# Talking heads: mixed heads copied in two halves by two engines, scaling on GpSimd, mixing and scores interleaved

## The chip, the cores and the metric

One core of a Trainium2 chip runs the whole program in one launch. The metric is the device time of one execution in microseconds, lower being better. Five engines work from queues of their own and meet at semaphores only: TensorE (PE; its weight loads are listed as PEld), VectorE (DVE), ScalarE (ACT), GpSimd (POOL) and SyncE (SP, which issues most DMAs).

## What is computed

The reference runs five layers over 16 images, each with 36 patch tokens and 512 text tokens of width 192: patch embedding, a kernelised attention, a gated attention, attention with talking heads, and a mixture of nine experts. The change touches the fourth layer alone, after a layer norm and with a residual around it:

```python
attn = jnp.einsum("bhnd,bhmd->bhnm", q, k) * scale
attn = jnp.einsum("gh,bhnm->bgnm", th1_w, attn) + th1_b[None, :, None, None]
attn = jax.nn.softmax(attn, axis=-1)
attn = jnp.einsum("gh,bhnm->bgnm", th2_w, attn) + th2_b[None, :, None, None]
out = jnp.einsum("bhnm,bhmd->bhnd", attn, v)
```

There are 12 heads of width 16. Scores are mixed over the heads before the softmax (th1) and after it (th2), all in float32.

## The kernel before

The layer is the function `talking_heads` (from line 1811). It walks over 16 images of 550 rows (548 tokens and padding), each cut into 55 tiles of 10 queries, so 880 tiles. One loop over STEPS (line 1875) is written out on every engine: image b, place i of 0 to 54, tile n = 55 b + i. The work of one tile on its way:

- GpSimd, `qg` (L1956), one step ahead: the queries times th1 for each of the 12 output heads, in two instructions (two halves of 5 queries). Three buffers (SB = 3).
- TensorE, scores (L2273): queries times keys, 24 matmuls of 274 columns into two banks of PSUM, for tile n + 3 in step n.
- VectorE: the largest value of a row (max, L2070) and from it the bias of the exponential (nb, L2073), for tile n + 2.
- ScalarE: the exponential (L2162) out of PSUM into `P`, with the row sums `rs`.
- VectorE: the reciprocal of `rs` (L2083), and the scaling (L2087): the mixing matrix of th2 times that reciprocal, 60 columns, into `mixn`, for tile n + 1.
- TensorE, mixing (L2259): `P` as weights against `mixn`, 40 matmuls of 60 columns into two banks of PSUM (MB and MB + 1, one for each half of the queries), which turns the probabilities as well.
- ScalarE: one copy of both banks (L2152), 600 elements a partition, into `P2`. The mixing of the next tile waits for it (`p2_in`, L2250).
- TensorE, after each of six groups of tiles (places ENDS: 8, 17, 26, 35, 44, 54): the product with the values, 120 matmuls (L2298); VectorE takes its sums (oT, L2095).

The scores' banks are three pairs, handed out in order; `wait_bank` (L1891) makes TensorE wait until what was in a pair three uses ago has been taken.

Eleven places of an image carry items of the neighbouring images (SLOTS, L1818): Y (output projection of the image before), X, Q, K, V (norm and projections of the image after), R and L (turned tokens and logits for the experts). TensorE does an item after the scores of that step; VectorE empties Y, Q, K and L in its following step (`take`, L2032), ScalarE the others. VectorE also does the statistics of the next image's norm (L1981, L1984, L1989) at places 0 to 5 and of the last norm at places 9 to 14, and the normalisations (L1992) at 6, 7, 9, 10, 11, 15, 16 and 18. GpSimd raises their variances to the power -1/2 (L1963 at place 5, L1966 at place 14), once VectorE has signalled them.

On VectorE a step reads: max and nb of tile n + 2, the takes of the step before, reciprocal and scaling of tile n + 1, oT, statistics and normalisations. On ScalarE: the copy of tile n, the exponential of tile n + 2, its items. On GpSimd: `qg` of tile n + 4, then the powers. On TensorE: mixing of tile n, scores of tile n + 3, item, values.

Of the kernel before, what the change touches and what calls it, by code (L numbers as in the profile page):

```python
# [28 lines left out]
T = 5  # L29
# [19 lines left out]
QT = 10  # L49
QG = 9  # L50
NG = 5
# [1759 lines left out]
def talking_heads(k, A, logits, tokens, turned, wz, bz, xz):  # L1811
# [11 lines left out]
    with ExitStack() as ctx:  # L1823
# [25 lines left out]
        ready, gapped = sem("ready"), sem("gapped")  # L1849
# [41 lines left out]
        def wait_bank(eng, u):  # L1891

            for part, m in uses[u - SB] if u >= SB else ():
                if part == "T":
                    eng.wait_ge(prob, m + 1)
                elif part == "Z":
                    eng.wait_ge(summed, m + 1)
                else:
                    eng.wait_ge(taken[part[0]], count(part, m))
                    if part[0] == "Q":  # L1900
                        eng.wait_ge(spread, count(part, m))

# [6 lines left out]
        with nc.Block() as block:  # L1909
# [27 lines left out]
            def _(pool):  # L1937
# [8 lines left out]
                for b, i, n in STEPS:  # L1946
                    m = n + SB + 1
                    if is_tile(m):
# [11 lines left out]
                        ins.then_inc(qg_in, 1)  # L1960
                    if i == 5 and 0 <= b < B - 1:
# [11 lines left out]
            def _(dve):  # L1973
# [91 lines left out]
                for b, i, n in STEPS:  # L2065
                    if is_tile(n + 2):
# [5 lines left out]
                        dve.wait_ge(largest, m + 1)  # L2072
                        dve.tensor_scalar(nb[:, p:p + 1], nmx[:, p:p + 1], b1[:, 0:1], b1[:, 0:1], ALU.subtract, ALU.add) \  # L2073
                           .then_inc(bias, 1)
                    if before:
                        for part, im in items(*before):
                            if part[0] in "YQKL":
                                take(part, im, item_at[before])
                    if is_tile(n + 1):
# [24 lines left out]
            def _(act):  # L2104
# [66 lines left out]
            def _(pe):  # L2171
# [68 lines left out]

                TAIL = {"Y03": 4, "Ra": 7, "La": 1}
# [3 lines left out]
                for b, i, n in STEPS:  # L2245
                    if is_tile(n):
                        p = n % SB
                        pe.wait_ge(scaled, n + 1)
                        if n:
                            pe.wait_ge(p2_in, n)  # L2250
                        else:
                            pe.wait_ge(gapped, 2)
                        if i == 0 and b:
                            spare(SPARE[min(b, 2)], p)
                        for t in range(T):
                            for a in range(2):
                                for s in range(2):
                                    q = slice(64 * s, 64 * s + HQ + 1)
                                    ins = pe.matmul(PS[64 * a:64 * a + KP, MB + s, t * HQ:(t + 1) * HQ], P[q, p, a, t * KP:(t + 1) * KP],  # L2259
                                                    mixn[q, p], start=True, stop=True)  # L2260
                        ins.then_inc(mixed, 1)
                    if is_tile(n + SB):
                        m = n + SB
                        p, bank, im = m % SB, 2 * (tile_at[m] % SB), m // NTILE
                        pe.wait_ge(qg_in, m + 1)
                        if m % NTILE == 0:
                            pe.wait_ge(taken["K"], count("K2", im))
                        wait_bank(pe, tile_at[m])
                        for c in range(NC):
                            for a in range(2):  # L2270
                                s = slice(a * PC, (a + 1) * PC)
                                for o, w in ((0, 64), (64, MR)):
# [598 lines left out]
```

## Time and profile before

| | us |
|---|---|
| median of 3 runs (lowest, highest) | 4380.58 (4378.49, 4381.98) |
| the profiled execution | 4380.37 |
| its span, first to last instruction | 4378.6 |
| PE busy in the span | 4176.6 (95%) |
| PEld, DVE, ACT, POOL busy | 3286.3, 2534.3, 2188.3, 1717.9 |

Times in a timeline are microseconds from the first instruction. A line joins neighbouring instructions of one kind; the number after the engine's idle time in brackets names what ended it, and "issue" stands for idle time that no semaphore in the profile explains. Matmuls overlap, and their ends are modelled: a start is exact, an end is not. In the groups by line, the number after the busy time is the mean of one instruction in ns.

### The profile page before, as it was taken

What the parts mean: (1) busy time and instruction counts of PE and PEld (TensorE: products, weight loads), DVE (VectorE), ACT (ScalarE), POOL (GpSimd) and SP (SyncE); (2) the same over time, 40 slices, a digit from 0 to 9 for tenths busy, and PEclk for the clock granted to TensorE, in tenths of its full rate; (3) what the DMA queues carried; (4) which work ended last, traced back from release to release, by engine and by line L of the source; (5) the groups of instructions that cost most, each with busy time, mean ns of one, the idle gap of its engine ahead of it and who ended that gap; (6) DMA issues with size and microseconds to landing.
All of it is one profiled execution on the core that took longest, in us unless ns stands there. A gap on an engine that the chain in (4) does not pass through costs nothing. (4 is left out here: it accounts for less than half of the span.)

```text
span 4378.6 us, 201182 instructions
## 1 busy us (share of the span) xinstructions
PE 4176.6 (95%) x88202; PEld 3286.3 (75%) x88202; DVE 2534.3 (58%) x7273; ACT 2188.3 (50%) x5051; POOL 1717.9 (39%) x2794
## 2 busy tenths in 40 slices
PE   6998998999989999999999999999999999999998
PEld 4555665766657777777877877787778777999997
DVE  5776886666655655566565556555655554432332
ACT  3453443555536555555555555555555553213443
POOL 2223435776743333333333333333333331002565
PEclk8999999999999999999999999999999999999999
DMA  5112210000000000100000000000000001332333
GB/s 114 25 34 47 48 33 7 1 2 1 1 14 4 16 5 14 24 16 4 16 16 16 4 16 16 16 4 16 16 16 4 16 16 38 77 88 65 66 67 50
DMA packets 122908, 114.73 MB, mean 26 GB/s; under 512 B 64000, under 2 KB 110594, under 8 KB 122042
## 3 DMA queue, kind: packets, MB, share of 16 engines
q1 hardware_dynamic: 94646, 66.47, 6.5%
q0 software_dynamic: 16768, 23.59, 3.0%
q10 hardware_dynamic: 10628, 11.80, 1.2%
q8 instruction: 706, 11.57, 1.1%
q14 instruction: 160, 1.31, 0.1%
HBM read 59.89 MB, written 41.48 MB: 23 GB/s over the span
## 5 line engine op out<-in xcount | busy, mean ns | idle before, releaser
L2273 PE MATMUL PS<-th_kT,th_qg 64*61 64x274 f32 (+1 forms) x21120 | 1461.1, 393 | 9.4 <-issue 7.0
L1956 POOL TENSOR_TENSOR th_qg<-th_qT,w_th_th 128x180 f32<-128x180 f32 x1760 | 849.9, 505 | 1355.6 <-PE PS L2273 1344.3
L2152 ACT ACTIVATE th_P<-PS 119x600 f32<-119x600 f32 x880 | 649.6, 738 | 849.9 <-PE PS L2259 849.5
L2273 PEld LDWEIGHTS PS<-th_kT,th_qg 64*61 64x61 f32 (+1 forms) x21120 | 879.8, 132 | 204.5 <-issue 35.2
L2070 DVE TENSOR_REDUCE th_nmx<-PS 125x1 f32<-125x548 f32 x880 | 640.3, 728 | 632.5 <-PE PS L2273 632.0
L2259 PEld LDWEIGHTS PS<-th_mixn,th_P 61*55 61x55 f32 x35200 | 672.6, 125 | 173.4 <-issue 66.9
L2259 PE MATMUL PS<-th_mixn,th_P 61*55 61x60 f32 x35200 | 708.0, 214 | 48.3 <-issue 40.4
L2162 ACT ACTIVATE th_P<-PS,th_nb 125x548 f32<-125x548 f32 x880 | 623.1, 708 | 105.7 <-DVE th_nb L2073 105.5
L1388 POOL TENSOR_SCALAR ga_P<-ga_P,ga_rw 110x110 f32<-110x110 f32 (+4 forms) x240 | 264.9, 1115 | 160.5 <-DVE ga_rw L1556 159.7
L2073 DVE TENSOR_SCALAR th_nb<-th_nmx,w_th_b 125x1 f32<-125x1 f32 x880 | 240.2, 273 | 32.2
L2298 PE MATMUL PS<-th_P,th_v 119*32 119x90 f32 (+1 forms) x11520 | 250.4, 244 | 1.1 <-ACT th_P L2152 0.8
L2298 PEld LDWEIGHTS PS<-th_P,th_v 119*32 119x32 f32 x11520 | 229.6, 110 | 29.1 <-issue 27.9
L2087 DVE TENSOR_SCALAR th_mixn<-w_th_mix,th_rs 125x60 f32<-125x60 f32 x880 | 233.0, 265 | 31.6
L2508 POOL DMA_INDIRECT ex_cx<-ex_tokens,ex_token_of x77 | 80.6, 1046 | 340.7 <-DVE ex_b L2685 250.7
L1617 ACT ACTIVATE ga_PT<-PS 110x440 f32<-110x440 f32 (+3 forms) x240 | 102.5, 427 | 198.3 <-PE PS L1702 196.1
L1030 PE MATMUL PS<-w_pf_wK,pf_xT 64*110 64x456 f32 x960 | 196.9, 557 | 1.5 <-ACT pf_xT L925 1.5
L2447 ACT ACTIVATE ez_h<-PS,ex_bz 128x550 f32<-128x550 f32 x96 | 69.0, 720 | 241.2 <-PE PS L2711 241.2
L2523 POOL DMA_INDIRECT out_h<-ex_cy,ex_token_of x77 | 130.6, 1697 | 132.1 <-DMA out_h<-ex_cy,ex_token_of 111.6
L2162 ACT ACTIVATION_READ_ACCUMULATOR th_P<-PS,th_nb 125x1 f32 x880 | 177.6, 202 | 0.0
L1079 PE MATMUL PS<-w_pf_wQ,pf_xT 64*110 64x360 f32 x960 | 166.9, 480 | 10.8 <-DVE X L901 6.4
L2434 ACT ACTIVATE ez_h<-PS,ex_cb 128x128 f32<-128x128 f32 x462 | 127.8, 376 | 77.5 <-PE PS L2782 75.8
L2772 PE MATMUL PS<-ex_cxT,ex_wz 64*128 64x128 f32 x2772 | 165.2, 275 | 1.0 <-ACT ez_h L2434 1.0
(369 smaller groups left out, 6291.8 us busy)
## 6 DMA issues: line engine op xcount, KB each, us to landing
pf_xT<-pf_spill SPq DMA_DIRECT2D x32, 412.5 KB, 5.5
ex_tokens<-th_xn SPq DMA_DIRECT2D x124, 82.5 KB
pf_spill<-pf_xT SPq DMA_DIRECT2D x16, 412.5 KB, 3.7
ex_turned<-th_rT SPq DMA_DIRECT2D x16, 412.5 KB, 3.7
ex_x<-ex_turned SPq DMA_DIRECT2D x32, 206.2 KB, 4.1
out_h<-X SPq DMA_DIRECT2D x16, 330.0 KB
ex_w<-in_L_ffn_W ACTq DMA_DIRECT2D x18, 288.0 KB
ex_w<-in_L_ffn_W ACTq DMA_DIRECT2D x8, 576.0 KB
```

The costliest lines, as they stand in the source:

```text
L1030: ins = pe.matmul(PS[0:R, p + a, 0:HM + D], xT[half, slot(u), c, cols(u)], wK[half, c, :], start=c == 0, stop=c == NC - 1)
L1079: ins = pe.matmul(PS[0:R, p + a, 0:HM + C], xT[half, qslot(u), c, cols(u)], wQ[half, c, :], start=c == 0, stop=c == NC - 1)
L1388: pool.tensor_scalar(P[:, n % 4, u, 0:keys(t)], P[:, n % 4, u, 0:keys(t)], rw[:, n % 4, u:u + 1], None, ALU.mult).then_inc(scaled, 1)
L1956: ins = pool.tensor_tensor(qg[:, m % SB, :, 64 * s:64 * s + HQ].rearrange("p c (h n) -> p c h n", n=QH), qT[:, im % 2, :, at + s * QH:at + ...
L2070: dve.tensor_reduce(nmx[:, p:p + 1], PS[0:MR, bank:bank + 2, 0:HK], AX.XY, ALU.max, negate=True) \
L2073: dve.tensor_scalar(nb[:, p:p + 1], nmx[:, p:p + 1], b1[:, 0:1], b1[:, 0:1], ALU.subtract, ALU.add) \
L2087: dve.tensor_scalar(mixn[:, p], mix[:], rs[:, p:p + 1], None, ALU.mult).then_inc(scaled, 1)
L2152: act.activation(P2[:, :, :, at * QT:(at + 1) * QT].rearrange("p t h (s n) -> p s (t h) n", s=2), PS[0:PK, MB:MB + 2, 0:VO].rearrange("p s ...
L2162: act.activation(P[:, p, :, 0:HK], PS[0:MR, bank:bank + 2, 0:HK], ACT.Exp, bias=nb[:, p:p + 1], accum_out=rs[:, p:p + 1]).then_inc(prob, 1)
L2259: ins = pe.matmul(PS[64 * a:64 * a + KP, MB + s, t * HQ:(t + 1) * HQ], P[q, p, a, t * KP:(t + 1) * KP], mixn[q, p], start=True, stop=True)
L2273: ins = pe.matmul(PS[o:w, bank + a, 0:HK], qg[s, p, c, o:w], kT[s, im % 2, c, :], start=c == 0, stop=c == NC - 1)
L2298: ins = pe.matmul(PS[32 * j:32 * j + 32, bank, c * nq:(c + 1) * nq], v[0:PK, b % 2, t].rearrange("p h d -> p (h d)")[:, at:at + 32], P2[:, ...
```

## The change

Four things change in `talking_heads`. The copy of the mixed heads becomes two: ScalarE copies bank MB, the first 5 queries, and VectorE bank MB + 1, the other 5; both wait for the mixing (and, at the first tile of a group, for the last value product) through the new helper `part_of`, and TensorE waits for both (`p2_in` and the new `p2_half`) before the next mixing and before the value product. The scaling goes from VectorE to GpSimd, behind the query product of the step. On VectorE the reciprocal now stands ahead of nb, and the takes stand behind the half copy. On TensorE, mixing and scores of a step are cut: key blocks 0 to 2 of 5 of the mixing, chunk 0 of 3 of the scores, blocks 3 and 4 of the mixing, chunks 1 and 2 of the scores. Matmuls, buffers and DMAs are the same.

```diff
+        def part_of(eng, n):
+
+            g = min(n % NTILE // QG, NG)
+            at = n % NTILE - g * QG
+            eng.wait_ge(mixed, n + 1)
+            if at == 0 and n:
+                eng.wait_ge(pv, n // NTILE * GROUPS + g)
+            return at
...
@@ gpsimd @@
                         ins.then_inc(qg_in, 1)
+                    if is_tile(n + 1):
+                        m = n + 1
+                        p = m % SB
+                        pool.wait_ge(recip, m + 1)
+                        if m >= SB:
+                            pool.wait_ge(mixed, m - SB + 1)
+                        pool.tensor_scalar(mixn[:, p], mix[:], rs[:, p:p + 1], None, ALU.mult).then_inc(scaled, 1)
                     if i == 5 and 0 <= b < B - 1:
...
@@ vector @@
                            .then_inc(largest, 1)
-                        dve.wait_ge(largest, m + 1)
-                        dve.tensor_scalar(nb[:, p:p + 1], nmx[:, p:p + 1], b1[:, 0:1], b1[:, 0:1], ALU.subtract, ALU.add) \
-                           .then_inc(bias, 1)
-                    if before:
-                        for part, im in items(*before):
-                            if part[0] in "YQKL":
-                                take(part, im, item_at[before])
                     if is_tile(n + 1):
                         m = n + 1
                         p = m % SB
                         dve.wait_ge(prob, m + 1)
                         dve.reciprocal(rs[:, p:p + 1], rs[:, p:p + 1]).then_inc(recip, 1)
-                        dve.wait_ge(recip, m + 1)
-                        if m >= SB:
-                            dve.wait_ge(mixed, m - SB + 1)
-                        dve.tensor_scalar(mixn[:, p], mix[:], rs[:, p:p + 1], None, ALU.mult).then_inc(scaled, 1)
+                    if is_tile(n + 2):
+                        m = n + 2
+                        p = m % SB
+                        dve.wait_ge(largest, m + 1)
+                        dve.tensor_scalar(nb[:, p:p + 1], nmx[:, p:p + 1], b1[:, 0:1], b1[:, 0:1], ALU.subtract, ALU.add) \
+                           .then_inc(bias, 1)
+                    if is_tile(n):
+                        at = part_of(dve, n)
+                        dve.tensor_copy(P2[:, :, :, at * QT + QH:(at + 1) * QT].rearrange("p t h n -> p (t h) n"),
+                                        PS[0:PK, MB + 1, 0:VO].rearrange("p (x n) -> p x n", n=QH)).then_inc(p2_half, 1)
+                    if before:
+                        for part, im in items(*before):
+                            if part[0] in "YQKL":
+                                take(part, im, item_at[before])
...
@@ scalar @@
-                        g = min(n % NTILE // QG, NG)
-                        at = n % NTILE - g * QG
-                        act.wait_ge(mixed, n + 1)
-                        if at == 0 and n:
-                            act.wait_ge(pv, n // NTILE * GROUPS + g)
-                        act.activation(P2[:, :, :, at * QT:(at + 1) * QT].rearrange("p t h (s n) -> p s (t h) n", s=2),
-                                       PS[0:PK, MB:MB + 2, 0:VO].rearrange("p s (x n) -> p s x n", n=QH), ACT.Copy).then_inc(p2_in, 1)
+                        at = part_of(act, n)
+                        act.activation(P2[:, :, :, at * QT:at * QT + QH].rearrange("p t h n -> p (t h) n"),
+                                       PS[0:PK, MB, 0:VO].rearrange("p (x n) -> p x n", n=QH), ACT.Copy).then_inc(p2_in, 1)
...
@@ tensor: the two loops become helpers mix_pieces(n, pieces) and score_pieces(m, chunks) @@
                         pe.wait_ge(scaled, n + 1)
                         if n:
                             pe.wait_ge(p2_in, n)
+                            pe.wait_ge(p2_half, n)
...
-                        for t in range(T):
-                            for a in range(2):
-                                for s in range(2):
...
-                        ins.then_inc(mixed, 1)
+                        mix_pieces(n, range(0, 3))
                     if is_tile(n + SB):
...
                         wait_bank(pe, tile_at[m])
-                        for c in range(NC):
...
-                        ins.then_inc(score, 1)
+                        score_pieces(m, range(0, 1))
+                    if is_tile(n):
+                        mix_pieces(n, range(3, T)).then_inc(mixed, 1)
+                    if is_tile(n + SB):
+                        score_pieces(n + SB, range(1, NC)).then_inc(score, 1)
...
                         pe.wait_ge(p2_in, n + 1)
+                        pe.wait_ge(p2_half, n + 1)
```

## Rows read from the trace of the kernel before

**Rows 1.** busy time by stretch: us, each engine's busy time (count), PEclk, DMA, GB/s

```profile
1290.50:3662.50 2372.00, 2312.35 (x70512) 1855.27 (x70514) 1397.68 (x4275) 1349.67 (x2822) 881.10 (x1784) 1.00 0.05 13
```

**Rows 2.** timeline, one step: start us, us, engine, line, operation, count, [idle before]

```profile
2035.68 0.71 PE L2259 MATMUL PS<-th_mixn,th_P 61*55 61x60 f32 x40
2035.94 0.73 DVE L2070 TENSOR_REDUCE th_nmx<-PS 125x1 f32<-125x548 f32 x1 [1.70 <-PE PS L2273]
2036.21 1.58 PE L2273 MATMUL PS<-th_kT,th_qg 64*61 64x274 f32 x24
2036.47 0.74 ACT L2152 ACTIVATE th_P<-PS 119x600 f32<-119x600 f32 x1 [1.18 <-PE PS L2259]
2036.71 0.27 DVE L2073 TENSOR_SCALAR th_nb<-th_nmx,w_th_b 125x1 f32<-125x1 f32 x1
2036.90 0.15 DVE L2083 RECIPROCAL th_rs<-th_rs 125x1 f32<-125x1 f32 x1
2037.09 0.25 DVE L2087 TENSOR_SCALAR th_mixn<-w_th_mix,th_rs 125x60 f32<-125x60 f32 x1
2037.25 0.35 DVE L1981 BATCH_NORM_STATS2 th_st<-X 110x6 f32<-110x192 f32 x1
2037.60 0.71 PE L2259 MATMUL PS<-th_mixn,th_P 61*55 61x60 f32 x40
```

**Rows 3.** who waited for whom, weight loads: us, times, longest

```profile
PEld PS L2259 <- issue: 66.9, 147, 1.4
PEld PS L2273 <- issue: 35.2, 80, 1.5
```

**Rows 4.** timeline: mixing of a step 27, scores of a step 9

```profile
2104.46 0.59 PE L2259 MATMUL PS<-th_mixn,th_P 61*55 61x60 f32 x28 [0.29 <-issue]
2206.38 0.20 PEld L2273 LDWEIGHTS PS<-th_kT,th_qg 64*64 64x64 f32 x7 [0.30 <-issue]
```

**Rows 5.** DMA queues of the page: packets, MB, share

```profile
q8 instruction: 706, 11.57, 1.1%
```

**Rows 6.** groups by shape, ACT, DVE and GpSimd: busy us, mean ns, idle before

```profile
L2128 ACT ACTIVATE th_v<-PS 128x192 f32<-128x192 f32 x16 | 5.3, 331 | 15.1 <-PE PS L2217 15.1
L2054 DVE COPY th_kT<-PS 128x274 f32<-128x274 f32 x15 | 6.7, 444 | 13.8 <-PE PS L2224 13.8
L2052 DVE COPY th_kT<-PS 128x548 f32<-128x548 f32 x15 | 10.9, 729 | 33.3 <-PE PS L2224 32.3 <-PE PS L2207 0.9
L2095 DVE TENSOR_TENSOR th_oT<-PS,w_th_one 128x180 f32<-128x180 f32 x80 | 27.7, 346 | 133.1 <-PE PS L2298 133.1
L1388 POOL TENSOR_SCALAR ga_P<-ga_P,ga_rw 110x110 f32<-110x110 f32 x48 | 27.4, 582 | 42.0 <-DVE ga_rw L1556 42.0
```

**Rows 7.** timeline, steps 5 to 7: GpSimd, scaling, mixing of tile 7

```profile
2048.31 1.17 POOL L1963 TENSOR_TENSOR th_rstd<-th_ve,mhalf 110x5 f32<-110x5 f32 x1 [5.60 <-DVE th_ve L1989]
2049.45 1.95 POOL L1956 TENSOR_TENSOR th_qg<-th_qT,w_th_th 128x180 f32<-128x180 f32 x4
2049.61 0.85 DVE L2087 TENSOR_SCALAR th_mixn<-w_th_mix,th_rs 125x60 f32<-125x60 f32 x1
2050.51 0.70 PE L2259 MATMUL PS<-th_mixn,th_P 61*55 61x60 f32 x36 [0.21 <-DVE th_mixn L2087]
```

**Rows 8.** timeline, step 4: mixing after slot 3, take of Y03

```profile
2044.33 0.75 PE L2259 MATMUL PS<-th_mixn,th_P 61*55 61x60 f32 x40
2044.44 0.96 DVE L2037 TENSOR_TENSOR X<-PS,X 110x768 f32<-110x768 f32 x1 [1.70 <-PE PS L2195]
```

**Rows 9.** timeline, steps 14 to 16: mixing, variance, power, mixing

```profile
2070.82 0.75 PE L2259 MATMUL PS<-th_mixn,th_P 61*55 61x60 f32 x40
2071.58 0.17 DVE L1989 TENSOR_SCALAR th_ve<-th_mv 110x5 f32<-110x5 f32 x1
2071.83 1.17 POOL L1966 TENSOR_TENSOR th_rstd<-th_ve,mhalf 110x5 f32<-110x5 f32 x1 [3.48 <-DVE th_ve L1989]
2074.71 0.70 PE L2259 MATMUL PS<-th_mixn,th_P 61*55 61x60 f32 x40
```

More of the change, by code:

```diff
@@ L1847, in sem @@
             return nc.alloc_semaphore("th_" + name)
-        ready, gapped = sem("ready"), sem("gapped")
+        ready, gapped, p2_half = sem("ready"), sem("gapped"), sem("p2_half")
         var, powed, xn_in = sem("var"), sem("powed"), sem("xn_in")
@@ L2239, in stream, with mix_pieces, score_pieces @@
                         pe.matmul(PS[:, bank, 0:2 * D], ident[0:C, :], wk[0:C].rearrange("p c n -> p (c n)"), start=True, stop=True)
+                def mix_pieces(n, pieces):
+                    p = n % SB
+                    for t in pieces:
+                        for a in range(2):
+                            for s in range(2):
+                                q = slice(64 * s, 64 * s + HQ + 1)
+                                ins = pe.matmul(PS[64 * a:64 * a + KP, MB + s, t * HQ:(t + 1) * HQ], P[q, p, a, t * KP:(t + 1) * KP],
+                                                mixn[q, p], start=True, stop=True)
+                    return ins
+                def score_pieces(m, chunks):
+                    p, bank, im = m % SB, 2 * (tile_at[m] % SB), m // NTILE
+                    for c in chunks:
+                        for a in range(2):
+                            s = slice(a * PC, (a + 1) * PC)
+                            for o, w in ((0, 64), (64, MR)):
+                                ins = pe.matmul(PS[o:w, bank + a, 0:HK], qg[s, p, c, o:w], kT[s, im % 2, c, :],
+                                                start=c == 0, stop=c == NC - 1)
+                    return ins
                 TAIL = {"Y03": 4, "Ra": 7, "La": 1}
@@ L2246, in _ @@
                     if is_tile(n):
-                        p = n % SB
                         pe.wait_ge(scaled, n + 1)
@@ L2253, in _ @@
                         if i == 0 and b:
-                            spare(SPARE[min(b, 2)], p)
-                        for t in range(T):
-                            for a in range(2):
-                                for s in range(2):
-                                    q = slice(64 * s, 64 * s + HQ + 1)
-                                    ins = pe.matmul(PS[64 * a:64 * a + KP, MB + s, t * HQ:(t + 1) * HQ], P[q, p, a, t * KP:(t + 1) * KP],
-                                                    mixn[q, p], start=True, stop=True)
-                        ins.then_inc(mixed, 1)
+                            spare(SPARE[min(b, 2)], n % SB)
+                        mix_pieces(n, range(0, 3))
                     if is_tile(n + SB):
                         m = n + SB
-                        p, bank, im = m % SB, 2 * (tile_at[m] % SB), m // NTILE
                         pe.wait_ge(qg_in, m + 1)
                         if m % NTILE == 0:
-                            pe.wait_ge(taken["K"], count("K2", im))
+                            pe.wait_ge(taken["K"], count("K2", m // NTILE))
                         wait_bank(pe, tile_at[m])
-                        for c in range(NC):
-                            for a in range(2):
-                                s = slice(a * PC, (a + 1) * PC)
-                                for o, w in ((0, 64), (64, MR)):
-                                    ins = pe.matmul(PS[o:w, bank + a, 0:HK], qg[s, p, c, o:w], kT[s, im % 2, c, :],
-                                                    start=c == 0, stop=c == NC - 1)
-                        ins.then_inc(score, 1)
+                        score_pieces(m, range(0, 1))
[3 more added lines that the diff above has]
+                        score_pieces(n + SB, range(1, NC)).then_inc(score, 1)
                     if (b, i) in item_at:
```

## The prediction, made before the change was run

> **What bounds the kernel now.** I read the busy times by stretch first, then one step in order of time, then who waits for whom, then prices. [...]
>
> The plain step shows how near the others are [rows 2]. Mixing starts at 2035.68, the scores at 2036.21, the next mixing at 2037.60: 0.53 us of mixing, 1.39 of scores, 1.92 in all; 880 such tiles are 1690 us, the items of the slots and the value products the rest. With 0 at the start of mixing, the max starts at 0.26, nb at 1.03, the reciprocal at 1.22, the scaling at 1.41, ending at 1.66; ScalarE's copy runs from 0.79 (0.26 after the mixing is out) to 1.53. The next VectorE instruction can start 0.09 before the one ahead of it ends (the scaling ends at 2037.34, statistics start at 2037.25). Both releases of the next mixing come only 0.26 to 0.39 us ahead of it.
>
> The list of waits gives the holes that are there: the weight loads of mixing sat idle 66.9 us and those of the scores 35.2 us for "issue", no semaphore at all [rows 3]. The trace has them within a block: 0.29 us ahead of the last 28 of 40 mixing matmuls in a step 27, 0.30 in the middle of the scores' weight loads in a step 9 [rows 4]. PE's instruction stream comes in 706 transfers of 11.57 MB, 16 KB each [rows 5]; I take these holes for late instructions. At most 102 us is to be had from them.
>
> **The change, part by part.**
>
> *Plain step: 0.* ScalarE's half is 300 elements: between 192 at 0.33 us [rows 6] and 600 at 0.74 [rows 2], 0.42. VectorE's half is like the 274-element copy at 0.44 [rows 6]: 0.47. GpSimd's scaling of 60 columns isn't in the trace; its nearest rows are 0.25 on VectorE [rows 2] and 0.58 for GpSimd's 110 columns [rows 6]; I take 0.45, nearer the row of that engine. TensorE's pieces are 0.32, 0.46, 0.21 and 0.93, still 1.92 together. The last mixing is out at 0.99, so both copies start at 1.25: ScalarE's half ends at 1.67. VectorE does max, reciprocal, nb (0.26 + 0.73 + 0.07 + 0.19 = 1.25), then its half until 1.72, free for the next at 1.63. The reciprocal now ends near 1.1, GpSimd's scaling at 1.6, earlier than VectorE's 1.66. Against 1.92 there is 0.20 left for the half; where the scaling was waited for, mixing came 0.05 after its end [rows 7], so I count 0.1 as slack. The cover is thin: without it a plain step pays up to 0.05, and 44 steps without an item in each of 16 images are 700. Bounds 0 to +35 us; 0 taken, since 0.20 is over 0.05.
>
> *Steps after an item: +2.2 us an image.* Here VectorE also empties an item's banks (take). Before, that stood ahead of the reciprocal and ran while the mixing did: Y03's add began at 2044.44 beside the mixing of 2044.33 [rows 8]. Now it stands behind the half, which waits for this tile's last mixing; queued behind that wait are the take, the sums of the values (oT), the statistics and the next max. They begin at 1.63 after the mixing's start, and the next max is due at 0.26 + 1.92 = 2.18: with T of such work it is T - 0.55 late. The half after it is as late, and with 0.1 of slack TensorE stalls T - 0.65, before the mixing three steps behind the item. Y03: 0.96 - 0.09 [rows 8] and statistics of 0.35 [rows 2] (0.27 and 0.08 for their sum): T 1.22, 0.57. Q0, Q1, Q2: two copies of 0.44 [rows 6] and a bubble, 0.92; after Q0 and Q2 also oT, 0.35 - 0.09 [rows 6]: 0.53, 0.27, 0.53. K01 with La: 0.73 - 0.09 [rows 6] and 0.09: 0.08. Together 1.98. Step 9 would lose 0.5 in the same way (Y4, oT, statistics, a normalisation: 1.16), but it has a hole of 0.3 of its own [rows 4]: 0.21, and without that cover 0.51. K2 with Lb and oT is 0.36, 0.09 and 0.26, hardly over 0.65: left out. Sum 2.19.
>
> *GpSimd's queue: +1.24 us an image.* The scaling now waits for VectorE's reciprocal, and behind it stands the next query product, two instructions, 0.96; 1.41 a step in 1.92 is no bound, and the products have three buffers. Not so where the powers stand in the queue. Step 5: the power starts at 2048.31, lasts 1.17, the product of the next step runs until 2050.41 [rows 7]; the scaling for tile 7 then ends at 2050.86 and mixing starts at 2050.91, not at 2050.51, where it now waits for a VectorE scaling stretched to 0.85 by the side of GpSimd's product [rows 7]: +0.40, and 0.04 as VectorE is later. Step 14: the statistics stand behind the half of a tile whose mixing starts at 2070.82 [rows 9]; half from 2072.07, last statistics at 2072.45, the variance 0.21 later, the power 0.25 after that (as 2071.58 to 2071.83), the product 1.14 on, 0.96 and 0.45 long: 2075.46, mixing of tile 16 at 2075.51 and not 2074.71 [rows 9]: +0.80. SP's queue is not passed; GpSimd issues no DMA here until the stage ends.
>
> *Weave: -8 us.* It moves no work, but mixing takes 80 instructions (40 matmuls [rows 2] and their weight loads) in 0.53 us and the scores 48 in 1.39. In the last two fifths of the mixing, TensorE's queue can now fill during the first third of the scores. Two fifths of 66.9 are 27 us; a third of that is gained, as the instruction transfers stay as long. Bounds 0 (nothing) to -68 (two thirds of all 102).
>
> [...]
>
> *Other waits.* One more semaphore for TensorE before mixing and before the value products: both stand after ScalarE's, at work of 1.72 against 1.92 (0). ScalarE gains 0.3 a step, off the path (0).
>
> **Sum.** (2.19 + 1.24) x 15 images = +51. Step 27, which Q0 would delay by 0.53, has the hole of [rows 4] in it: -0.3 x 15 = -5. Weave -8. Net +38. The profiled execution took 4380.37 us (its span of 4378.6 and 1.8 around it), 0.2 below the median of the runs, so 4380.4 + 38 = **4418 us**.
>
> **Rivals.**
> 1. *Faster: the holes for instructions close.* They are set by how densely mixing eats instructions; the weave puts 64 into each half of a step, the stream keeps up, -55 of the 102 comes back, and half of the new waits fall where holes were (+25): 4350 (4337 at -68, 4357 at -48). It decides once the weave saves more than the waits cost. For it: holes lie within mixing [rows 4]. Against: the same 128 instructions per 1.92 us, transfers of the same length.
> 2. *No change.* The late VectorE work falls into holes that are there, and only GpSimd's +1.24 x 15 = 19 is left, less 8 to 20 of the weave: 4380 to 4391, 4384. For it: holes of 102 us are as large as all new waits. Against: the new ones come at steps of their own, and of those reckoned here only steps 9 and 27 showed a hole.
> 3. *Slower still.* The half gates plain steps too: 0.25 from its end to the mixing and not 0.1 gives 0.05 x 700 = 35: 4453. For it: 0.20 of room. Against: the 0.05 of [rows 7].
> 4. The change not doing what it says would be a mixing that still waits for one 600-element copy; the diff leaves none.
>
> **How the numbers follow.** Forecast (4395 to 4438) 0.50, rival 1 0.21, rival 2 0.13, rival 3 0.16. About 0.2% (9 us) is what a measurement can tell. Faster 0.21, same 0.12, and slower 0.67 (forecast, rival 3 and the top of rival 2). Range 4356 to 4454: it takes in the two slower cases, rival 2 and rival 1 up to its weaker end; the forecast's own is 4395 to 4438.
>
> **What would show it.** Right: mixing waits on VectorE's half after the steps of Y03, Q0 to Q2; the weight loads of mixing wait on GpSimd's scaling some 15 times after step 5 and 15 after step 14; plain steps stay at 1.92; "issue" idle of mixing and scores falls by under 30 us. Wrong: "issue" idle falling by over 50 (rival 1), or every plain step near 1.97 (rival 3), or GpSimd's scaling far from 0.45.

## The result, and the profile after

The changed kernel takes 4434.53 us (median of 4 runs, 4430.71 to 4436.11) against 4381.28 us of the kernel before beside it: ratio 1.0117, 95% interval 1.0105 to 1.0129. That is 53 us slower. The forecast was 4418 us, its range 4356 to 4454. Timed beside the kernel before on a second chip (4366 us there), the ratio was 1.0136, interval 1.0120 to 1.0153. All experiments below ran on chips where the kernel before took 4358 to 4366 us; they are compared by their ratios to it, the change itself at 1.0136. Its own ratio moved by 0.0019 from one chip to the other, so a smaller difference between two experiments (0.0019 is 8 us) decides nothing.

The profiled execution took 4436.11 us, 55.7 us more than that of before. The page's first lines, and the stage in the busy times by stretch (columns as in [rows 1]):

```profile
span 4434.4 us, 202173 instructions
PE 4225.1 (95%) x88202; PEld 3238.4 (73%) x88202; DVE 2655.3 (60%) x7273; ACT 1943.2 (44%) x5051; POOL 2065.0 (47%) x3674
```

```profile
1290.50:3718.50 2428.00, 2361.26 (x70535) 1806.62 (x70535) 1515.09 (x4276) 1104.89 (x2822) 1232.12 (x2667) 1.00 0.05 12
```

The stage went from 2372.00 [rows 1] to 2428.00 us, so the whole loss is in it, at the same granted clock of 1.00. ScalarE gave up 245 us of work, VectorE took 117 and GpSimd 351. The groups by line price the three new instructions, which were estimated at 0.45, 0.42 and 0.47 us:

```profile
L1976 POOL TENSOR_SCALAR th_mixn<-w_th_mix,th_rs 125x60 f32<-125x60 f32 x880 | 384.9, 437 | 1161.5 <-DVE th_rs L2092 1089.9
L2167 ACT ACTIVATE th_P<-PS 119x300 f32<-119x300 f32 x880 | 403.8, 459 | 1182.6 <-PE PS L2262 1182.6
L2101 DVE COPY th_P<-PS 119x300 f32<-119x300 f32 x880 | 414.1, 471 | 611.2 <-PE PS L2262 606.8
```

A plain step, to be laid beside [rows 2] (timeline; mixing is now L2262, scores L2272):

```profile
2171.99 0.52 PE L2262 MATMUL PS<-th_mixn,th_P 61*55 61x60 f32 x24
2172.26 0.73 DVE L2086 TENSOR_REDUCE th_nmx<-PS 125x1 f32<-125x548 f32 x1 [0.45 <-PE PS L2272]
2172.31 0.67 PE L2272 MATMUL PS<-th_kT,th_qg 64*64 64x274 f32 x8
2172.78 0.41 PE L2262 MATMUL PS<-th_mixn,th_P 61*55 61x60 f32 x16
2172.90 0.15 DVE L2092 RECIPROCAL th_rs<-th_rs 125x1 f32<-125x1 f32 x1
2172.99 1.13 PE L2272 MATMUL PS<-th_kT,th_qg 64*64 64x274 f32 x16
2173.15 0.43 POOL L1976 TENSOR_SCALAR th_mixn<-w_th_mix,th_rs 125x60 f32<-125x60 f32 x1 [0.69 <-DVE th_rs L2092]
2173.26 0.43 ACT L2167 ACTIVATE th_P<-PS 119x300 f32<-119x300 f32 x1 [0.78 <-PE PS L2262]
2173.26 0.48 DVE L2101 COPY th_P<-PS 119x300 f32<-119x300 f32 x1
2173.59 0.71 ACT L2177 ACTIVATE th_P<-PS,th_nb 125x548 f32<-125x548 f32 x1
2173.92 0.27 PE L2262 MATMUL PS<-th_mixn,th_P 61*55 61x60 f32 x5
```

The pieces start at 0, 0.32, 0.79 and 1.00, the half ends at 1.75, the next mixing comes at 1.93. The plain step is as drawn. So the loss sits in particular steps, and the list of waits is the next view to read, beside [rows 3]:

```profile
PEld PS L2262 <- POOL th_mixn L1976: 109.6, 321, 1.3
PEld PS L2262 <- issue: 107.7, 415, 1.1
PEld PS L2272 <- issue: 63.2, 174, 1.3
PE PS L2262 <- issue: 22.2, 55, 0.9
PE PS L2262 <- POOL th_mixn L1976: 15.7, 27, 0.8
PE PS L2262 <- DVE th_P L2101: 3.6, 15, 1.1
```

It misleads three times. The 109.6 us on GpSimd's scaling are mostly the short idle time that a weight load has in any step whose last release is the scaling: in the run below in which no step is late for it, it is still 63.9. VectorE's half, which mixing was to wait for after the steps of Y03 and Q0 to Q2, is named 15 times only, ahead of place 11; in step 28, shown below, the list names the scaling, which ends 0.24 us before the next mixing starts, and the half ends only 0.15 before it. And the idle time for "issue", where a fall was forecast, rose from 66.9 to 107.7 us for the weight loads of mixing and from 35.2 to 63.2 for those of the scores [rows 3]; without the weave they are 49.3 and 34.3. For the scores, "issue" turns out to hide a semaphore.

What tells more is the length of each step, by its place in the image (from the start of one mixing to the next, in each trace; median over images 1 to 14, us; "all three" and the others are the experiments below):

```
place           24    33    42     5     6    15    28    10    38    30
before         1.92  1.94  1.92  1.92  2.30  1.92  1.92  2.09  1.92  1.92
after          2.21  2.21  2.21  2.45  2.90  2.84  2.43  2.37  2.38  1.93
no weave       1.92  1.92  1.92  1.98  2.90  2.38  1.97  1.92  1.92  1.92
takes early    2.21  2.21  2.21  2.23  2.86  2.84  1.93  2.10  2.09  1.93
power moved    2.21  2.21  2.21  2.23  1.93  2.21  2.43  2.44  2.24  1.93
early + power  2.21  2.21  2.21  2.23  1.93  2.26  1.93  2.17  2.10  1.93
but five       1.99  1.99  1.99  2.01  1.93  1.99  1.93  2.17  2.35  1.93
all three      1.92  1.92  1.92  1.92  1.92  1.92  1.92  1.92  1.92  1.92
```

Places 24, 33 and 42 grew by 0.27 to 0.29 us with no late work behind them. The timeline of place 24 of one image after, and then of the same place without the weave:

```profile
2118.92 0.71 ACT L2177 ACTIVATE th_P<-PS,th_nb 125x548 f32<-125x548 f32 x1
2119.28 0.49 PE L2262 MATMUL PS<-th_mixn,th_P 61*55 61x60 f32 x24
2119.52 0.20 ACT L2177 ACTIVATION_READ_ACCUMULATOR th_P<-PS,th_nb 125x1 f32 x1
2119.83 0.23 PEld L2272 LDWEIGHTS PS<-th_kT,th_qg 64*64 64x64 f32 x8 [0.19 <-issue]
2119.86 0.69 PE L2272 MATMUL PS<-th_kT,th_qg 64*64 64x274 f32 x8
```

```profile
2094.35 0.71 ACT L2177 ACTIVATE th_P<-PS,th_nb 125x548 f32<-125x548 f32 x1
2094.95 0.20 ACT L2177 ACTIVATION_READ_ACCUMULATOR th_P<-PS,th_nb 125x1 f32 x1
2095.18 0.70 PE L2262 MATMUL PS<-th_mixn,th_P 61*55 61x60 f32 x40
2095.70 1.57 PE L2272 MATMUL PS<-th_kT,th_qg 64*64 64x274 f32 x24
```

Banks are handed out in turn, three pairs. The item of slot 22 takes one, so the scores of step 24 get the pair of the tile scored in step 22, two steps back and not three, and `wait_bank` waits for that tile's exponential. After the change this exponential ends 0.44 us after the mixing starts (2119.72), since it stands behind a half copy that starts only when the woven mixing is out; the first third of the scores is due at 0.32 and starts at 0.58. Without the weave the exponential ends at 2095.15, before the mixing, and the scores are due at 0.52. The same holds two steps behind every slot that carries an item without a value product: 3, 13, 22, 31, 40, so places 5, 15, 24, 33, 42.

### The profile page after: what moved, and what is told of

It is laid out like the page before. It is cut to its first block and busy times, and to the rows that moved or that the text cites. A ratio compares the mean times of both kernels' runs of the same rounds, so it can differ in the third digit from the quotient of the medians.

```text
span 4434.4 us, 202173 instructions
## 1 busy us (share of the span) xinstructions
PE 4225.1 (95%) x88202; PEld 3238.4 (73%) x88202; DVE 2655.3 (60%) x7273; ACT 1943.2 (44%) x5051; POOL 2065.0 (47%) x3674
## 3 DMA queue, kind: packets, MB, share of 16 engines
q8 instruction: 706, 11.57, 1.1%
## 5 line engine op out<-in xcount | busy, mean ns | idle before, releaser
L2272 PE MATMUL PS<-th_kT,th_qg 64*61 64x274 f32 (+1 forms) x21120 | 1648.7, 394 | 18.7 <-issue 12.5
L2262 PEld LDWEIGHTS PS<-th_mixn,th_P 61*55 61x55 f32 x35200 | 842.1, 125 | 328.5 <-POOL th_mixn L1976 109.6
L2262 PE MATMUL PS<-th_mixn,th_P 61*55 61x60 f32 x35200 | 904.2, 215 | 44.7 <-issue 22.2
L1976 POOL TENSOR_SCALAR th_mixn<-w_th_mix,th_rs 125x60 f32<-125x60 f32 x880 | 384.9, 437 | 1161.5 <-DVE th_rs L2092 1089.9
L2167 ACT ACTIVATE th_P<-PS 119x300 f32<-119x300 f32 x880 | 403.8, 459 | 1182.6 <-PE PS L2262 1182.6
L2272 PEld LDWEIGHTS PS<-th_kT,th_qg 64*61 64x61 f32 (+1 forms) x21120 | 767.2, 132 | 152.4 <-issue 63.2
L2101 DVE COPY th_P<-PS 119x300 f32<-119x300 f32 x880 | 414.1, 471 | 611.2 <-PE PS L2262 606.8
```

Of the source, the lines that this page charges most:

```text
L1976: pool.tensor_scalar(mixn[:, p], mix[:], rs[:, p:p + 1], None, ALU.mult).then_inc(scaled, 1)
L2101: dve.tensor_copy(P2[:, :, :, at * QT + QH:(at + 1) * QT].rearrange("p t h n -> p (t h) n"), PS[0:PK, MB + 1, 0:VO].rearrange("p (x n) -> ...
L2167: act.activation(P2[:, :, :, at * QT:at * QT + QH].rearrange("p t h n -> p (t h) n"), PS[0:PK, MB, 0:VO].rearrange("p (x n) -> p x n", n=Q ...
L2272: ins = pe.matmul(PS[o:w, bank + a, 0:HK], qg[s, p, c, o:w], kT[s, im % 2, c, :], start=c == 0, stop=c == NC - 1)
```

## The experiments

**Is it the weave?** In the changed kernel, mixing and scores are each in one piece again.

```diff
-                        mix_pieces(n, range(0, 3))
+                        mix_pieces(n, range(T)).then_inc(mixed, 1)
...
-                        score_pieces(m, range(0, 1))
-                    if is_tile(n):
-                        mix_pieces(n, range(3, T)).then_inc(mixed, 1)
-                    if is_tile(n + SB):
-                        score_pieces(n + SB, range(1, NC)).then_inc(score, 1)
+                        score_pieces(m, range(NC)).then_inc(score, 1)
```

> The changed kernel with the mixing of a tile in one piece again and the scores in one piece behind it; halves, GpSimd's scaling and the late takes stay. Theory A (the weave costs time): in the changed kernel the first third of the scores starts 0.32 us after the mixing and not 0.53, and at places 5, 15, 24, 33 and 42, two steps behind an item, it then waits some 0.27 us for the exponential that has its bank; and both half copies start 0.46 later, and all that stands behind them on VectorE with them. Without the weave the five waits go (1.35 us an image, 20 us over 15), the steps 5, 28 and 37 lose most of what they gained (about 1 us an image, 15 us), the power of place 14 starts 0.46 earlier (7 us), and some 7 us of instruction holes come back: 4434.5 - 35, about 4399. Theory B (as the prediction had it, the weave gains 8 us and costs nothing): 4442. Theory C (holes for instructions dominate): 4460 or more.

Measured: ratio 1.0028, interval 1.0017 to 1.0040, against 1.0136 for the whole change on such a chip: the weave costs 0.0108, 47 us (0.0089 or 39 against the first 1.0117), more than the 35 of theory A. Places 24, 33, 42, 10 and 38 are back at 1.92, 5 and 28 nearly so, place 15 fell by 0.46. Place 6 stays at 2.90: the power's. The takes of places 5, 10 and 28 stand as late in VectorE's queue as before and now cost 0.06 us at most: the mixing that they stand behind is out at 0.52 and not at 1.00. So here late takes cost only beside the weave, and the 47 us hold both.

**Is it the takes?** The takes move up, between nb and the half copy.

```diff
                            .then_inc(bias, 1)
+                    if before:
+                        for part, im in items(*before):
+                            if part[0] in "YQKL":
+                                take(part, im, item_at[before])
                     if is_tile(n):
                         at = part_of(dve, n)
...
-                    if before:
...
```

> The changed kernel with VectorE's takes (Y, Q, K, L) put between nb and the half copy instead of behind it. Theory A: the late takes cost what places 10 to 12, 28 and 37 gained and part of place 5 (about 1.3 us an image), the rest of the loss being bank waits of the weave and GpSimd's powers: 4434.5 - 20, about 4415, with places 24, 33 and 42 still at 2.21 us and place 15 at 2.84. Theory B (the prediction's: all 2.19 us an image are the takes'): 4434.5 - 33, about 4402. Theory C (the waits come from GpSimd's queue whatever VectorE does): 4434.

Measured: 1.0106, interval 1.0089 to 1.0123, 0.0030 or 13 us under the change (5 against the first 1.0117). Place 28 fell by 0.50, 10 by 0.27, 5 by 0.22; 24, 33, 42 and 15 stayed, as theory A had it. By places that is 1.0 us an image, 15 us, as the timing has it. Theory B's 33 us are out. Place 38 fell by 0.29 too, but not for its take: one pair of neighbouring instructions of TensorE there starts 0.66 us apart after the change, 0.35 with the takes early and 0.05 without the weave (means), a hole of the kind that the last experiments are about. Place 28 after the change shows how a late take costs (VectorE, TensorE and GpSimd; the Q0 of slot 26):

```profile
2130.82 0.47 DVE L2101 COPY th_P<-PS 119x300 f32<-119x300 f32 x1 [4.15 <-PE PS L2262]
2131.21 0.88 DVE L2061 COPY th_qT<-PS 64x275 f32<-64x275 f32 x2
2131.50 0.52 PE L2262 MATMUL PS<-th_mixn,th_P 61*55 61x60 f32 x24
2132.16 0.23 PEld L2272 LDWEIGHTS PS<-th_kT,th_qg 64*64 64x64 f32 x8 [0.27 <-issue]
2132.19 0.69 PE L2272 MATMUL PS<-th_kT,th_qg 64*64 64x274 f32 x8 [0.16 <-issue]
2132.38 0.72 DVE L2086 TENSOR_REDUCE th_nmx<-PS 125x1 f32<-125x548 f32 x1
2133.26 0.43 POOL L1976 TENSOR_SCALAR th_mixn<-w_th_mix,th_rs 125x60 f32<-125x60 f32 x1 [5.36 <-DVE th_rs L2092]
2133.32 0.46 DVE L2101 COPY th_P<-PS 119x300 f32<-119x300 f32 x1
2133.90 0.53 PEld L2262 LDWEIGHTS PS<-th_mixn,th_P 61*55 61x55 f32 x23 [0.37 <-POOL th_mixn L1976]
2133.93 0.63 PE L2262 MATMUL PS<-th_mixn,th_P 61*55 61x60 f32 x23
```

VectorE stood 4.15 us with the item's bank full, waiting for the mixing, and took it afterwards, until 2132.09. The scores of step 28 need that bank: due at 2131.82, they start at 2132.19. The late max then delays reciprocal, scaling and half as well, and the next mixing starts 0.15 after the half.

**Is it the power?** The statistics start earlier, so that GpSimd's powers fall into steps 3 and 13, in which TensorE has an item to do.

```diff
-                    if i == 5 and 0 <= b < B - 1:
+                    if i == 3 and 0 <= b < B - 1:
...
-                    if i == 14 and b >= 1:
+                    if i == 13 and b >= 1:
...
-                    if i <= T:
+                    if im == 0 and i <= T:
                         stat_of(im, 0, i)
+                    if im and i <= T - 2:
+                        stat_of(im, 0, i + 2)
...
-                    if 9 <= i <= 9 + T:
+                    if 8 <= i <= 8 + T:
...
-                        stat_of(im, 1, i - 9)
+                        stat_of(im, 1, i - 8)
...
+                    if b + 2 < B and i >= NTILE - 2:
+                        stat_of(b + 2, 0, i - NTILE + 2)
```

> The changed kernel with the statistics of the next norm two places earlier (53, 54, 0 to 3) and those of the last norm one place earlier (8 to 13), so that GpSimd's two powers of 1.2 us stand at places 3 and 13, steps of 5.1 and 3.7 us in which GpSimd idles, and not at 5 and 14. Theory A (the power stands ahead of a query product and the scaling, and mixing waits for that): place 6 falls from 2.90 to about 2.3 and place 15 from 2.84 to about 2.2 (the bank wait of 0.27 stays), 1.25 us an image: 4434.5 - 19, about 4415. Theory B (the late VectorE sets these steps, not the power): less than 6 us gained, 4429 or more.

Measured: 1.0100, interval 1.0080 to 1.0120, 0.0036 or 16 us under the change (7 against the first 1.0117). Place 6 fell to 1.93, place 15 to 2.21; places 10 and 16 grew by 0.07 and 0.20. What went is seen in step 15 after the change, beside [rows 9]:

```profile
2096.97 1.20 POOL L1982 TENSOR_TENSOR th_rstd<-th_ve,mhalf 110x5 f32<-110x5 f32 x1 [1.56 <-DVE th_ve L2005]
2098.14 0.97 POOL L1965 TENSOR_TENSOR th_qg<-th_qT,w_th_th 128x180 f32<-128x180 f32 x2
2099.09 0.51 POOL L1976 TENSOR_SCALAR th_mixn<-w_th_mix,th_rs 125x60 f32<-125x60 f32 x1
2099.65 0.40 PEld L2262 LDWEIGHTS PS<-th_mixn,th_P 61*55 61x55 f32 x24 [0.92 <-POOL th_mixn L1976]
```

Power, product, scaling, mixing: the queue that the prediction had drawn. The mixing before it started at 2096.81.

**All three together.** What is left of the change are the halves and the scaling on GpSimd.

> The three edits together: no weave, takes ahead of the half copy, powers at places 3 and 13. Halves and GpSimd's scaling are all that is left of the change. Theory A (the loss is those three and nothing else): 4381 give or take 8, that is no better than the kernel before, since the halves and the scaling on GpSimd shorten no step that TensorE bounds. Theory B (halves and GpSimd's scaling cost by themselves, in each plain step): 4395 or more. Theory C (shorter VectorE and ScalarE queues gain something once the rest is out of the way): 4370 or less.

Measured: 0.9978, interval 0.9968 to 0.9988, 4356.14 us against 4366.09; on the 4381 us from which the theories reckon that is 4372, just under theory A's 4373 and above theory C's 4370. Each of the ten places above is at 1.92, so the three edits hold the loss of these places; why the time is even below that of the kernel before is taken up with the last experiments. Here is the wait on the scaling that is left in a kernel in which it costs nothing:

```profile
PEld PS L2268 <- POOL th_mixn L1976: 63.9, 328, 1.2
```

**The change once more, and the weave with nothing else against it.** The changed kernel was timed again beside the next three runs; then the early takes and the moved powers with the weave kept.

> The changed kernel itself once more, so that it has been timed beside the kernel before on a second chip, on which the kernel before took 4366 us and not 4381. Theory A: the loss comes from waits between engines, at the same places of each image, and is 48 to 55 us here too (ratio 1.011 to 1.0125). Theory B: part of it is holes for instructions, which differ from chip to chip; then the ratio moves by more than 0.002.

Measured: 1.0136, interval 1.0120 to 1.0153; it differs from 1.0117 by 0.0019, just under the 0.002 that was to speak for theory B, and it lies above theory A's 1.011 to 1.0125: it decides for neither.

> The changed kernel with the takes ahead of the half copy and the powers at places 3 and 13; the weave stays. It differs from the run with all three edits (0.9978 of before) by the weave alone. Theory A (the weave costs five bank waits of 0.28 us an image, 21 us, and little else once the takes and the powers are out of its way): 0.9978 + 0.005, about 1.003. Theory B (the edits add up as they were measured one by one, -0.0011 and -0.0017 from 1.0117): 1.0089. Theory C (the weave costs nothing by itself): 0.998.

Measured: 1.0057, interval 1.0042 to 1.0072, between theories A and B. Takes and powers, worth 13 and 16 us one by one, are worth 34 together. The weave by itself costs 1.0057 - 0.9978 = 0.0079, another 34 us. The five places make 1.5 us an image of it, 23 us.

**Are the halves worth anything?** The run with all three edits, with ScalarE's single copy; and the kernel before with the powers moved.

```diff
-                        act.activation(P2[:, :, :, at * QT:at * QT + QH].rearrange("p t h n -> p (t h) n"),
-                                       PS[0:PK, MB, 0:VO].rearrange("p (x n) -> p x n", n=QH), ACT.Copy).then_inc(p2_in, 1)
+                        act.activation(P2[:, :, :, at * QT:(at + 1) * QT].rearrange("p t h (s n) -> p s (t h) n", s=2),
+                                       PS[0:PK, MB:MB + 2, 0:VO].rearrange("p s (x n) -> p s x n", n=QH), ACT.Copy).then_inc(p2_in, 1)
...
-                        dve.tensor_copy(P2[:, :, :, at * QT + QH:(at + 1) * QT].rearrange("p t h n -> p (t h) n"),
-                                        PS[0:PK, MB + 1, 0:VO].rearrange("p (x n) -> p x n", n=QH)).then_inc(p2_half, 1)
...
```

> The run with all three edits (no weave, early takes, moved powers), and ScalarE copies both banks again in one instruction, as before; VectorE has no half. What is left of the change is the scaling on GpSimd and the reciprocal ahead of nb. Theory A (ScalarE's copy was never the bound, the halves gain nothing): the same within 0.0012 as with halves, 0.9978. Theory B (the earlier exponential frees the scores' banks sooner, the halves gain): 1.000 or more. Theory C (VectorE's half ends 0.19 later than ScalarE's whole copy and holds work behind it, the halves cost): 0.996 or less.

> The kernel before with the statistics and the powers moved to places 3 and 13 and nothing else. In the kernel before only place 6 shows the power (2.30 us and not 1.92, VectorE's scaling stretched beside GpSimd's product). Theory A: 0.38 us an image is gained, 6 us, ratio 0.9987; then some 4 us of what the run with all three edits gained (0.9978) are from the scaling on GpSimd and the halves. Theory B: 0.9978, all of that gain is the moved power and nothing of it the change's. Theory C: no change, 1.000.

Measured: 1.0004 (0.9994 to 1.0013) and 1.0000 (0.9990 to 1.0010). At face value the halves would gain 0.0026, theory B's figure, and the scaling on GpSimd nothing. But between the run with the halves and the one without, the plain steps are alike (1.92), and places 0, 7, 8 and 17, which are 1.4 us shorter together with the halves, stand against 9, 11, 16 and 40, which are 1.4 longer (means). Most of this is holes that changed places, as the last two runs show them: 1.0 of the first 1.4 at places 0 and 7, 1.1 of the second at 9, 11 and 40. At place 16 the halves cost 0.26: VectorE's half, late behind two normalisations, ends 0.15 before the next mixing. With the powers moved in the kernel before, place 6 fell from 2.30 to 1.92; these 6 us do not show in its time.

**Is there room on VectorE for both?** All three edits, the scaling back on VectorE behind the reciprocal.

```diff
-                        pool.tensor_scalar(mixn[:, p], mix[:], rs[:, p:p + 1], None, ALU.mult).then_inc(scaled, 1)
...
                         dve.reciprocal(rs[:, p:p + 1], rs[:, p:p + 1]).then_inc(recip, 1)
+                        dve.wait_ge(recip, m + 1)
+                        if m >= SB:
+                            dve.wait_ge(mixed, m - SB + 1)
+                        dve.tensor_scalar(mixn[:, p], mix[:], rs[:, p:p + 1], None, ALU.mult).then_inc(scaled, 1)
...
```

> The run with all three edits (no weave, early takes, moved powers; 0.9978 of before), and the scaling back on VectorE, right behind the reciprocal; the halves stay. Theory A (VectorE has no room for both): in a plain step the max ends 0.99 after the mixing starts, the reciprocal 1.10, the scaling 1.35, nb 1.54, the half about 2.0, past the 1.92 of the step; some 700 plain steps grow by 0.15 us or a little more, 105 us and up: ratio 1.022 or more. Theory B (the half fits, since VectorE's chain shifts against TensorE's): 0.998 to 1.002, and the scaling need not have moved.

Measured: 1.0084, interval 1.0068 to 1.0099: 0.0106 or 46 us over the run with all three edits, in the direction of theory A and less than half its size. One step of its timeline:

```profile
2463.25 0.75 PE L2265 MATMUL PS<-th_mixn,th_P 61*55 61x60 f32 x40
2464.35 0.25 DVE L2093 TENSOR_SCALAR th_mixn<-w_th_mix,th_rs 125x60 f32<-125x60 f32 x1
2464.70 0.46 DVE L2106 COPY th_P<-PS 119x300 f32<-119x300 f32 x1
2465.31 0.75 PE L2265 MATMUL PS<-th_mixn,th_P 61*55 61x60 f32 x40
```

The half ends at 1.91, the next mixing starts 0.15 later, at 2.06. Only part of the plain steps are so long; place 30 is 2.09, places 24, 33 and 42 are 2.04, place 38 stays at 1.93. So VectorE can carry the half only once the scaling has left it; the two parts of the change belong together.

**Are the five places what the weave costs?** The run that kept the weave, unwoven at five places.

```diff
-                        mix_pieces(n, range(0, 3))
+                        cut = T if i in (5, 15, 24, 33, 42) else 3
+                        ins = mix_pieces(n, range(cut))
+                        if cut == T:
+                            ins.then_inc(mixed, 1)
...
-                    if is_tile(n):
-                        mix_pieces(n, range(3, T)).then_inc(mixed, 1)
+                    if is_tile(n) and cut < T:
+                        mix_pieces(n, range(cut, T)).then_inc(mixed, 1)
```

> The run with early takes and moved powers that kept the weave (1.0057 of before), with the weave undone at places 5, 15, 24, 33 and 42 alone. Theory A (there the scores' first third comes two steps behind an item, too early for the exponential that has its bank): these five steps fall from 2.21 to 2.32 us to some 1.93, 1.5 us an image, 22 us: 1.0057 - 0.005, about 1.0007; what is left of the weave's 0.0079 is 0.003. Theory B (the bank wait only stands where TensorE would wait anyway): 1.0045 or more.

Measured: 1.0095, interval 1.0082 to 1.0109: slower, where 1.0007 was expected. Yet the five places fell nearly as expected, to 1.99 to 2.01. In exchange place 17 grew by 0.98 us and place 44 by 1.01 (means). Step 17, PE alone:

```profile
2383.18 0.52 PE L2268 MATMUL PS<-th_mixn,th_P 61*55 61x60 f32 x21
2384.68 0.31 PE L2268 MATMUL PS<-th_mixn,th_P 61*55 61x60 f32 x3 [0.98 <-issue]
2384.81 0.69 PE L2278 MATMUL PS<-th_kT,th_qg 64*64 64x274 f32 x8
```

This is a hole of 1 us within one block of matmuls, where the kernel has no semaphore. I counted the starts of TensorE's instructions, semaphore instructions included. In this trace 75 gaps between neighbouring starts are over 0.4 us in images 1 to 14, and all 75 fall on the same position modulo 256, that is on cuts between the 16 KB transfers of [rows 5] (64 bytes an instruction, by 11.57 MB and the 180,758 instructions counted before). The packets of that queue show what is waited for: in every trace here, TensorE goes on after such a gap 1.19 to 1.68 us after a 16 KB transfer has landed, while about half of the cuts without a gap are crossed later than that. So the hole is a wait for instructions. Gaps over 0.25 us at these cuts add up to 76.5 us; in the run that kept the weave everywhere they were 59.0. So 15 us of bank waits were removed and 17.5 us of holes came up elsewhere; the timing (0.0038 more) is worse still, which these two profiles don't settle. By idle time of the mixing matmuls, first the run with the weave everywhere, then this one:

```profile
PE PS L2268 <- issue: 25.4, 73, 0.9
```

```profile
PE PS L2268 <- issue: 42.2, 91, 1.1
```

**Do the holes depend on the cuts alone?** All three edits, with 32 more and with 32 fewer one-column spare matmuls ahead of image 1.

```diff
-    SPARE = (39, 43, 14)
+    SPARE = (39, 75, 14)
```

(and 11 for 75).

> The run with all three edits (0.9978 of before), with 32 more one-column spare matmuls ahead of image 1, so that from there on TensorE's instruction stream is cut into its 16 KB transfers 64 instructions later in every image. Theory A (the holes without a semaphore are set by where these cuts fall): they leave places 9, 11, 13 and 40 and turn up elsewhere, and the time moves by more than 6 us one way or the other. Theory B (the holes belong to the places, whatever the cut): the same places and 0.9978 within 0.0014.

> The run with all three edits (0.9978 of before) with 32 fewer one-column spare matmuls ahead of image 1 (11 and not 43), so that the cuts between TensorE's instruction transfers come 64 instructions earlier; with 32 more it was 1.0017. Theory A (any shift moves the holes; the three points scatter by more than 0.003, so that a difference of 0.2% between kernels whose instruction streams are cut differently says nothing of the edit): outside 0.9978 give or take 0.0014 in either direction. Theory B (0.9978 is what the schedule is worth and the run with 32 more was the odd one): within it.

Measured: 1.0017 (1.0007 to 1.0027) and 1.0007 (0.9998 to 1.0016). The two expectations speak of 64 instructions. The traces have 64 more and 64 fewer matmuls, each with a weight load, so the cuts moved by 128 instructions, half a transfer, forward and back, and that is the same place: 450 of 490 cuts fall on the same instruction of the same step in both, none where the run with all three edits has one, and the holes agree (place 18 at 2.94 us in both, 1.96 with all three edits alone). This is one shift, timed twice. With 32 more, place 9 falls from 2.82 to 1.96 us, 11 from 2.37 to 1.92 and 40 from 6.05 to 5.34 (medians), while holes turn up at 12, 18 and 39. So the holes go with the cuts: theory A, of the first run. Shifting the cuts, with no other edit, moves the time by 0.0029 to 0.0039, 13 to 17 us; the three runs were timed on three chips, and how much of that is the chip's is not shown. So 0.9978 is a good draw: the same schedule with its cuts elsewhere gives 1.0017 and 1.0007. The run with all three edits was measured faster than both kernels, but by no more than the place of its cuts explains; I claim no gain for halves and scaling.

## Why the prediction was right or wrong

The sign and the range were right; of the sum, 38 us were forecast and 53 (58 on the second chip) measured. Step by step:

- **Plain step: right.** Durations were within 0.04 us. The median went from 1.920 to 1.927 with the weave and not with all three edits; 0.007 over 44 steps of 15 images is about 5 us that was not counted. The slack between half and mixing is 0.15 (the run with VectorE's scaling), not 0.1, and 0.18 was there. Rival 3 (1.97) is out.
- **Steps after an item: right in kind, too large.** 2.19 us an image, 33 us, were counted; taking early gave 13 us by time and 15 by places. Y03 was put at 0.57 and the takes' part is 0.22; Q0 was 0.53 and gave 0.50, though the scores' wait for the item's own bank was not in the working; step 9's work was 0.21 and gave 0.27 at place 10. Q1 (0.27), Q2 (0.53) and K01 (0.08) gave nothing: places 33 and 42 did not move when the takes did, and place 37, where Q2's stall was due, went from 2.31 to 2.29. That 33 grew by 0.27, just as forecast for Q1, and 5 by 0.53, near Y03's 0.57, is luck: all of the one and 0.31 of the other are the wait for a bank.
- **GpSimd's queue: right.** 1.24 us an image was forecast (0.44 and 0.80), and moving the power took 0.60 off place 6 beyond its old hole, and 0.63 off place 15: 1.23. That the sum agrees so well is luck, one part being 0.16 more and the other 0.17 less. With the old hole of place 6 the two make 24 us, of which the time shows 16.
- **Weave: wrong in sign, the main error.** It stood at -8 with bounds 0 to -68, and the runs give +34, and +47 with the late takes in the same kernel. The third of 27 us behind the -8 was an estimate of mine that no run shows. The step that failed is the sentence "it moves no work": it moves the moment at which the scores ask for their banks, 0.21 earlier, and the moment at which the exponential frees them later. The wait at the front of the scores was quoted from the code and never set against the exponential's end. The bound "nothing" on the slow side had no row behind it. The five places are 23 of the 34 us. The rest is not taken apart; 0.007 us a plain step (5 us) and gaps at the cuts (59.0 us against 53.0) are in it. The 13 us beyond 34 are those of the takes: the prediction counted them in full at the mixing's end of the weave, 0.99, and booked nothing of them on the weave.
- **Holes for instructions.** Rival 1 would have closed them. They did not close: gaps over 0.25 us at the cuts were 71.1 us before and 62.3 after, 55.5 us in the change timed again and 50.1 without the weave, 59.0 and 53.0 in the other pair. Of some 490 cuts in images 1 to 14 only 83 to 135 had a gap over 0.25 us, and still these made 46 to 77 us in all in each trace here. The 5 us of step 27 were no gain either: its hole stayed (2.39 and 2.46 us, means), and Q0's stall came a step later, at place 28.

Two errors hid each other: the takes were 18 to 20 us too dear, the weave 42 too cheap, and the time came within 17 us. The closeness is luck: without the weave, whose cost it did not see, the same kernel is 12 us slower (1.0028) and not the 46 that its other terms come to.

## What to carry to other kernels

Weaving two blocks of one engine moves no work, but it moves each block's first instruction and last result; list every semaphore that the two ends touch, and look for the steps in which a rotation of buffers is shorter than usual, since a plain step shows nothing of it (here 1.92 us before and 1.93 after, while places 24, 33 and 42 grew by 0.27 to 0.29). Work behind a copy that waits for the late engine is late itself: empty banks before such a wait, price the parts of a change together (here late takes cost 13 us beside the weave and next to nothing without it), and keep long rare instructions (here a power of 1.2 us) out of a queue that has just become part of the path. A difference of 0.3% between builds whose instruction streams are cut differently is no verdict on an edit until the cuts have been shifted (here, with no other edit, the ratio moved by 0.0029 to 0.0039).

## What the runs showed of the hardware that was not expected

In these traces TensorE's holes without a semaphore went with the cuts in its instruction stream: 75 of 75, 66 of 66 and 55 of 56 gaps over 0.4 us fell on one position modulo 256 in three of the runs (the weave undone at five places, 32 spare matmuls fewer, 32 more). They reached 1.35 us there, ended 1.19 to 1.68 us after the landing of a 16 KB transfer, turned up after a small retiming elsewhere in the image (0.98 us more at place 17, 1.01 at place 44), and changed places when the cuts were shifted by 128 instructions, half a transfer (place 18 went from 1.96 to 2.94 us, place 9 from 2.82 to 1.96); shifts of 128 forward and of 128 back had the same holes. With such a shift the time of one schedule changed by 13 to 17 us of 4366, the chip's part in that unknown. What decides whether a given cut is late stays open.
